# A 48-job attention pipeline: loop written out, row loads moved in the DMA queue, places of side work renumbered

## The reference, cut to what matters

```python
for i in range(6):                                   # x: (4, 512, 256), 16 heads of 16
    xn = adaln(x, cond, n1_w[i], n1_b[i])            # layer norm, then scale and shift from cond
    q, k, v = split(xn @ qkv_w[i].T, 3)              # self attention
    x = x + attn(rope(q), rope(k), v) @ so_w[i].T
    xn = adaln(x, cond, n2_w[i], n2_b[i])            # cross attention on ctx (4, 512, 256)
    q, k, v = xn @ cq_w[i].T, ctx @ ck_w[i].T, ctx @ cv_w[i].T
    x = x + attn(rope(q), rope(k), v) @ co_w[i].T
    xn = adaln(x, cond, n3_w[i], n3_b[i])
    x = x + gelu(xn @ f1_w[i].T + f1_b[i]) @ f2_w[i].T + f2_b[i]     # 256 -> 1024 -> 256
# then, on x0 + x: a mixture of 8 experts (top 2, capacity 640, 256 -> 512 -> 256), added to x
```

## Time and profile before

| what | us |
|---|---|
| median of 3 runs | 4334.48 (4331.78 to 4341.4) |
| the profiled execution | 4337.09 |
| its span, first to last instruction | 4335.3 |
| PE busy | 3833.6 (88% of the span) |
| DVE, ACT, POOL busy | 2841.1, 2498.6, 1148.4 |
| mean granted clock of TensorE | 0.966 of 2.4 GHz |
| SHORT slot in the loop / written out | 63.1 / 62.8 |
| LONG slots | 96.0 to 102.3 |
| everything after the last attention slot (from 3990.6) | 344.7 |

### The profile page before, as it was taken

How to read it: one execution, slowest core, us unless ns; L and a number is a source line. 1 busy time by engine, 2 the same in 40 slices (tenths; PEclk the granted TensorE clock), 3 DMA queues, 4 the chain that set the end, 5 groups by cost and what they waited for, 6 DMA issues and landing times. The chain is left out here.

```text
span 4335.3 us, 66534 instructions
## 1 busy us (share of the span) xinstructions
PE 3833.6 (88%) x19478; PEld 1695.2 (39%) x19478; DVE 2841.1 (66%) x4476; ACT 2498.6 (58%) x4206; POOL 1148.4 (26%) x1280
## 2 busy tenths in 40 slices
PE   3899899899899899899999899999999999897558
PEld 1233344433344433344433344433344433343446
DVE  6788766688666688766688766588766688751411
ACT  1577655577655567655567655567655577654112
POOL 3233222232222232322232322232322232301043
PEclk8999999999999999999999999999999999999779
DMA  5655534445533355433356443456443366521235
GB/s 160 157 153 145 131 80 94 107 137 145 131 81 91 97 145 141 132 90 82 93 150 148 125 95 82 94 145 153 123 99 80 91 171 154 132 54 46 68 103 112
DMA packets 334220, 500.30 MB, mean 115 GB/s; under 512 B 53705, under 2 KB 242257, under 8 KB 333521
## 3 DMA queue, kind: packets, MB, share of 16 engines
q1 hardware_dynamic: 289680, 430.95, 39.0%
q0 software_dynamic: 44160, 64.73, 6.3%
HBM read 278.54 MB, written 222.58 MB: 116 GB/s over the span
## 5 line engine op out<-in xcount | busy, mean ns | idle before, releaser
L908 ACT ACTIVATE prob<-ps 128x512 f32<-128x512 f32 x3072 | 1751.3, 595 | 1249.8 <-PE ps L832 1246.9
L1070 DVE TENSOR_REDUCE negmax<-ps 128x2 f32<-128x1024 f32 x1536 | 1814.8, 1217 | 362.4 <-PE ps L859 332.5
L832 PE MATMUL ps<-qstack,kstack 114*128 114x512 bf16 x3072 | 1144.6, 390 | 118.0 <-ACT prob L908 99.0
L845 PE MATMUL psv<-prob,v 128*32 128x512 f32 x6144 | 826.7, 610 | 0.0
L832 PEld LDWEIGHTS ps<-qstack,kstack 114*128 114x128 bf16 x3072 | 273.9, 97 | 1269.3 <-ACT prob L908 935.7
L859 PE MATMUL ps<-kstack,qstack 49*128 49x512 bf16 x3072 | 487.8, 387 | 78.7 <-DVE negmax L1070 53.3
L677 POOL TENSOR_TENSOR pool_fence<-eps 128x1 f32<-128x1 f32 x288 | 55.2, 192 | 1688.0 <-ACT mrow L975 1026.5
L807 PE MATMUL side<-nT,wf 128*128 128x256 f32 x1536 | 375.0, 387 | 31.9 <-ACT mrow L975 18.3
L1106 DVE TENSOR_SCALAR hT<-side,f1b 128x256 f32<-128x256 f32 x384 | 167.5, 478 | 295.6 <-PE side L807 295.5
L818 PE MATMUL side<-wf,hT 128*128 128x256 f32 x1536 | 350.1, 381 | 3.5 <-DVE x L1113 1.8
L807 PEld LDWEIGHTS side<-nT,wf 128*128 128x128 f32 x1536 | 285.4, 191 | 88.2 <-ACT mrow L975 22.3
(11 more groups left out here) (170 smaller groups left out, 3626.8 us busy)
## 6 DMA issues: line engine op xcount, KB each, us to landing
bounce<-parts SPq DMA_DIRECT2D x480, 256.0 KB, 2.5
qstack<-bounce SPq DMA_DIRECT2D x384, 192.0 KB, 6.1
kstack<-bounce SPq DMA_DIRECT2D x384, 192.0 KB, 6.6
value_sums<-osum SPq DMA_DIRECT2D x192, 256.0 KB, 6.5
bounce<-low SPq DMA_DIRECT2D x96, 256.0 KB, 2.1
hT<-value_sums POOLq DMA_DIRECT2D x96, 256.0 KB, 4.8
nT<-inverse POOLq DMA_DIRECT2D x96, 256.0 KB, 3.8
ctxT<-in_ctxT SPq DMA_DIRECT2D x24, 512.0 KB, 5.3
```

The source lines that it names most:

```text
L832: nc.tensor.matmul(ps2[:, n % RING2, :], kk[0:ROWS, h, kt * P:(kt + 1) * P], q[0:ROWS, h, :], start=True, stop=True).then_inc(s_p2full, 1)
L845: mm = nc.tensor.matmul(psv[32 * i:32 * i + 32, 0, :], v[j % 2][:, kt, (HD + 1) * h:(HD + 1) * h + 32], prob[:, 4 * (u % 2) + i, :], start ...
L908: nc.scalar.activation(prob[:, 4 * (u % 2) + i, :], ps2[:, n % RING2, :], ACT.Exp, scale=HD ** -0.5).then_inc(s_prob, 1)
L1070: nc.vector.tensor_reduce(out_at, ps1[:, 2 * (n % 2):2 * (n % 2) + 2, :], AX, ALU.max, negate=True).then_inc(s_p1free, 1)
```

## The change

Five things change, and what is computed stays the same.

1. `run_slots` writes all 50 slots out; every wait has a constant, and `Place` is gone.
2. The parts: `bounce` has four rows for Q (high, high, mid, low) and four for K (low, mid, high, high). `load_first` and `load_second` read three neighbouring rows each, so a job needs 8 writes, not 12.
3. SP's queue: half 1 of job k is loaded in slot k, behind a new wait for `s_aload`, that is until the chain of job k-2 has loaded everything. The weights come behind those rows: cross weights at k % 8 = 2, F1's at 3, F2's at 4, self weights at 6.
4. POOL: `waited` and `pool_fence` are gone (288 instructions).
5. The tables of places.

```diff
 SHORT = {
-    "M": [25, 0], "HV": [1, 3], "HT": [6, 8], "HQ": [9, 11], "HK": [12, 14], "O": [18, 20],
-    "SPLIT": (14, 16, 19, 21), "PARTS": 23, "RECIP": 8, "NORM": (14, 15),
+    "M": [25, 0], "HV": [1, 3], "HT": [6, 7], "HQ": [8, 9], "HK": [12, 14], "O": [18, 20],
+    "SPLIT": (12, 14, 18, 20), "PARTS": 23, "RECIP": 6, "NORM": (10, 11),
 LONG = {
-    "M": [27, 0], "HV": [1, 3], "HT": [6, 8], "O": [11, 12], "HQ": [14, 15], "HK": [16, 18], "LT": [17, 19],
-    "F1": [20, 21, 22, 23, 24, 25, 26, 27], "F2": [28, 29, 30, 31],
-    "SPLIT": (17, 19, 21, 23), "GELU": (24, 28), "PARTS": 25, "RECIP": 5, "NORM": (9, 10),
+    "M": [27, 0], "HV": [1, 3], "HT": [6, 7], "HQ": [8, 9], "O": [11, 12], "HK": [13, 15], "LT": [16, 17],
+    "F1": [18, 19, 20, 21, 22, 23, 24, 25], "F2": [26, 28, 30, 31],
+    "SPLIT": (13, 15, 18, 20), "GELU": (22, 26), "PARTS": 24, "RECIP": 5, "NORM": (8, 9),
-    "LN_LT": dict(stats=[12, 12, 12, 12], aggregate=13, guess=13, newton=14, tiles=[14, 14, 15, 15]),
+    "LN_LT": dict(stats=[12, 12, 12, 12], aggregate=13, guess=14, newton=14, tiles=[14, 14, 15, 15]),
...
-Q_PARTS = (0, 0, 1, 0, 1, 2)
-K_PARTS = (0, 1, 0, 2, 1, 0)
+PART_ORDER = ((0, 0, 1, 2), (2, 1, 0, 0))
+FIRST_AT, SECOND_AT = (0, 1), (1, 0)
...
-    with eng.Fori(0, NL - 1) as layer:
-        place.layer = layer
-        for k in range(2, 2 + NJ):
-            slot(k, p2=True, p1=True, tail=True, head=True)
...
+    for k in range(JOBS + 2):
+        slot(k, p2=1 <= k <= JOBS, p1=k < JOBS, tail=k >= 2, head=k + 1 < JOBS)
...
                 if tail:
                     write_sums(k - 2, 3)
-                if k % NJ == 2 and p1:
-
-                    sp.wait_ge(s_full, side_done)
-                    load_cross_ffn(k)
                 if head and is_cross(k + 1):
...
+                if tail and p1:
+
+                    sp.wait_ge(s_aload, 64 * (k - 1))
+                if k and p1:
+                    load_first(k, 1)
+                    load_second(k, 1)
+
+                if k % NJ == 2 and p1:
+
+                    sp.wait_ge(s_full, side_done)
+                    load_cross(k)
+                if k % NJ in (3, 4) and p1:
+                    load_ffn(k, k % NJ - 3)
...
-                if head:
-                    load_first(k + 1, 1)
-                    load_second(k + 1, 1)
...
-                wait_sums(pool, place, j)
-                waited()
+                wait_sums(pool, j)
                 pool.dma_start(den[:, :], sums[j % 2][:, HD].rearrange("h (c n) -> h c n", c=P // H)).then_inc(s_den, 16)
```

More of the change, by code:

```diff
@@ L463, in layers @@
         number, start = {}, {}
-        for k in range(-1, 2 * NJ + 2):
+        for k in range(-1, JOBS + 2):
             start[k] = len(number)
@@ L501, in _ @@
         def _(sp):
-            place = Place()
             def at_layer(name, k):
-                layer = place.layer + k // NJ
-                ap = a[name]
-                return ap[bass.ds(layer, 1)] if not isinstance(layer, int) else ap[layer:layer + 1]
+                return a[name][k // NJ:k // NJ + 1]
             def load_self(k):
@@ L535, in write_part @@
-                sp.wait_ge((s_hi, s_mid, s_low)[part], place.jobs(j, 2) + w + 1)
-                for r in range(NPROD):
+                        sp.wait_ge(s_first[hf], FIRST_DMAS * j)
+                        sp.wait_ge(s_second[hf], SECOND_DMAS * j)
+                sp.wait_ge((s_hi, s_mid, s_low)[part], 2 * j + w + 1)
+                for r in range(len(order)):
                     if order[r] == part:
@@ L591, in slot @@
             def slot(k, p2, p1, tail, head):
[L592 removed]
+                side_done = start[k]
                 for g in NORM_WEIGHTS.get(k, {}):
@@ L1083, in side_work @@
                     return
-                wait_filled(dve, place, k, what, c)
+                wait_filled(dve, k, what, c)
                 bank = side[:, 0, :]
```

243 lines of the change are left out of this document (100 added, 143 removed).

## The result

The changed kernel takes **4213.3 us** (4208.2 to 4219.1, 4 runs) against 4333.9 (4331.8 to 4341.4), a ratio of 0.9719, 95% interval 0.9700 to 0.9738. So 121 us are gained where 194 were forecast, and the time lies above the range of 4100 to 4205. The profiled execution took 4208.2, its span is 4206.5.

What follows compares the result with a forecast made beforehand. PE was taken to set slot length, plus its idle times. Gains of 26.6 + 24 + 80.8 + 28.6 + 30 + 10 = 200 us off 4334.5 give 4134.5; with 5.5 given back, 4140 us, range 4100 to 4205.

Steps and rivals of the forecast that it cites:

- terms 4: Other LONG-slot places: M's copy 0.8 us, HQ/HK neighbours 0.3, LT's wait 0.2 gained; 28.6 us, bounds -20 and 58.
- Term 5: SHORT slots: PE's waits of 0.31 and 1.04 us behind ACT's casts go; 30 us, bounds 15 and 33.
- its check: Cross-check of the forecast time by slots: 24 SHORT slots at 61.5 us and 21 LONG at 92.5.
- Terms 1 and 2: Loop written out: waits at four layer turns go, 26.6 us; constants replace counts in registers, 24 us, bounds 14 and 34.
- Term 3: LONG slots: waits at RECIP and NORM go, and the clock's falls behind them; 80.8 us, or 40 if NORM still waits.
- the sign that the prediction gave for being wrong: In the trace after: lower clock in slots that have no wait of the attention's chain, one of several signs; no size given.
- Term 6: Half 1's row loads behind the chain arrive 2.6 us before pass 1 needs them in SHORT slots; cost nothing.
- rows late: Rival: half 1's rows come some 3 us late in 24 SHORT slots, costing 72 us, 4212; chance 0.10.
- straight code stalls: Rival: written-out code stalls 5.5 us in every fourth of 40 slots, giving back 55, 4195; chance 0.04.
- Term 7: Start and ends: slot 47's wait of 5.6 us shrinks, slots 0, 1 and 49 gain; 10 us, bounds 5 to 14.
- the chain stays too slow: Rival: a wait at NORM, place 8 or 10, remains; term 3 shrinks to 40, Term 7 to 5, 4186; chance 0.15.
- The give-back: 5.5 us returned from the gain for small waits of the 0.3 kind from new neighbours, 0.1 in a slot.

Runs made afterwards that it cites:

- Experiment 1: The kernel before with only the layer loop written out and waits on constants, places, parts and row loads as before: 4269.2 us, 0.9834 of the kernel before.
- Experiment 8: Changed kernel with K's chunks at 14 and 15, first cast at 12, guess at 13, all norm tiles at 14 in LONG slots: 4195.4 us, 0.9658.
- experiment 9: Changed kernel with LT at 17 and 18, F1 at 19 to 26, F2 at 28 to 31, gelus at 24 and 28 in LONG slots: 4171.7 us, 0.9596.
- experiment 2: Changed kernel with the old tables of places, all else of the change kept: 4231.6 us, 0.9750 of the kernel before.
- experiment 4: Changed kernel with DVE's two products (NORM) in SHORT slots back at places 14 and 15, not 10 and 11: 4263.1 us, 0.9822.
- (5): Changed kernel with DVE's two products (NORM) in SHORT slots at places 11 and 16, not 10 and 11: 4205.1 us, 0.9686.
- Experiment 7: Changed kernel with chunk M at 22 and the parts at 19 in SHORT slots, so the M rows load earlier: 4185.3 us, 0.9645.
- (11): Changed kernel with six rows of parts in DRAM as before, 192 more writes, all else as changed: 4213.2 us, 0.9703.
- Experiment 12: Changed kernel with M 22, parts 19, products 11 and 16 (SHORT), LT 17 and 18, F1 and F2 later, gelus 24 and 28 (LONG): 4129.4 us, 0.9489.

## Why the prediction was wrong, step by step

The step that failed is the same in terms 4 and 5: each moved step was priced by the wait that it takes away. What the moves add, beside a wait of 1.4 us at LT, was put at 0.1 us in a slot, 5.5 in all, with nothing for a fall of the clock behind them. The runs show 1.27 us in each SHORT slot (DVE's products behind a rope of Q), late M rows at the ends of ten, and 0.78 and 2.07 us in each LONG slot (DVE's tiles behind a rope of K), with a fall of the clock behind them in 19 of 21.

The profiled executions differ by 128.9 us, 65.6 less than the forecast's 194.5. The medians add 7.7 to the miss, since the profiled execution of before lies 2.6 above its median and that of after 5.1 below. The rest is this:

| part of the miss | us |
|---|---|
| SHORT slots without a late row, mostly the new wait, (62.4 - 61.5) x 24 | 21.6 |
| SHORT slots over 62.4 (late M rows, the clock behind) | 15.2 |
| falls of the clock in LONG slots, (94.05 - 92.64) x 19 | 26.8 |
| LONG slots without a fall, 0.14 x 21 | 2.9 |
| start and ends | 6.4 |
| given back already in the forecast, and rounding of its check | -7.2 |

**Terms 1 and 2, the loop.** The edges were right: no DVE wait on "issue" at a turn is left, and slot 10 takes 62.45 with the change. The counts in registers were too low: 41 us (67.8 of the spans less 26.6), outside the bounds of 14 to 34. The step that failed is the comparison of slots 15 and 46 behind LT: it measures how much slower the matmuls' stream is, but with 0.9 for a whole slot it leaves only 4 us for the stretch ahead of LT in all twenty. Experiment 1 shows the place: behind LT it gained 15.2 us, as counted (14), and ahead of LT 25.3. There the attention's chain runs; NORM's waits fall by 13 us, and three falls of the clock are gone. That it is the chain's own waits on counts is likely, not shown.

**Term 3, the chain.** The mechanism was right at both its places. RECIP's wait went by the order of SP's queue and NORM's by the places, and PE does not wait for the products ahead of O in any LONG slot of the loop. Sizes: 80.8 was worked out as all that lies over 94.7, and some of this was the loop's (above), so terms 2 and 3 counted in one sum are the better reading. They were forecast at 99 in LONG slots; with term 4 that makes the 127 of the table, against 97.4. DVE still idles at NORM in ten LONG slots of the loop, 0.2 to 1.45 us, but PE does not see it. The step that failed stands in its words "half what the clock costs behind them": the fall was taken to go with this wait, but it came back behind another. This is the sign that the prediction gave for being wrong: a lower clock in slots that have no wait of the chain.

**Term 4, other places in LONG slots.** M's copy: right, 18.3 to nothing. LT's wait was forecast at 1.4 and is 2.07, with 0.78 ahead of it; the step that followed DVE put the last two tiles at 0.7, and they took 1.67, since one of them stands until POOL's instruction beside it is over (last section). It also did not ask what DVE's backlog does to the scores ahead of LT. The two waits together are 1.4 us over the forecast, within the bound of 3.5. What it triggers was not in the bound at all: the fall of the clock in 19 slots, 26.8 us. Experiment 8 takes most falls away and gets 26 us back; experiment 9 halves them, shortens LT's wait as well, and gets 53 (a slot without a fall takes 91.4 there, not 92.6). That such a slot takes 92.64 in the changed kernel where 92.5 was forecast, in spite of 1.4 us more of these waits, is in part luck: small waits went that the sum did not have. With the old tables (experiment 2) slot 14 has 0.54 us for an exponential and 0.42 and 0.39 for ropes, and 0.3 was counted.

**Term 5, ACT's casts in SHORT slots.** The casts' waits went, 1.35 a slot. But the step asked only what covers ACT; the products that the same table moved from 14 and 15 to 10 and 11 stood only in the rivals, for whether the inverses are there in time, not for whom they hold up. They hold up PE for 1.27 us. SHORT slots gained 27.9 in all, and 26.6 of that is term 1: terms 2 and 5 came to about nothing there. That moving them back is worse (experiment 4) and moving them apart better (5) speaks for their distance from the ropes as what counts. What stood in no step: earlier casts bring half 0's row loads forward, and the M rows' load, whose place did not change, is then issued behind all ten of them, not amid them. Experiment 7 gets 32 us back, of which these waits themselves are 12.4. In experiment 2, with the old places, no SHORT slot has this wait.

**Term 6, half 1's row loads.** Right. In slot 13 (from 1019.2) SP issues the first at 1040.38, 21.2 us in (forecast 21.8), and PE passes unit 8 without a wait, 35.1 us in:

```profile
1033.82 0.58 POOL L658 DMA_DIRECT2D inverse<-recip  x1 [6.65 <-DVE recip L1119]
1040.38 0.32 SPq L525 DMA_DIRECT2D qstack<-bounce  x1
...
1054.32 0.60 PE L824 MATMUL ps<-kstack,qstack 49*128 49x512 bf16 x4
```

The four-row parts are worth nothing that can be told (11). The rivals "rows late" and "straight code stalls" did not come. That the first of them gives 4212 and 4213 was measured is chance: no PE wait for the rows of half 1 is there.

**Term 7, the ends.** 3.6 of 10. Slot 47 still has a wait for the inverses, which moved from O to NORM as the rival "the chain stays too slow" has it:

```profile
3711.37 0.69 DVE L1123 TENSOR_TENSOR hT<-hT,nT 128x512 f32<-128x512 f32 x1 [3.45 <-DMA nT<-inverse]
...
3713.25 0.61 PE L824 MATMUL ps<-kstack,qstack 49*128 49x512 bf16 x2 [3.72 <-DVE negmax L1027]
```

**The give-back and the range.** 5.5 us for "small waits that new neighbours bring" stood for what cost about 60 (21.6, 15.2 and 26.8 above). The sentence on the range gives "about 35 us to each side", and that does not follow from the bounds: their root of squares is 31 us on the side of more gain (10, 29.4 and 3) and 66 on the side of less (10, 40.8, 48.6 and 15). The stated range, 40 and 65 us from 4140, is near that. A root of squares takes the misses as apart, but the three large ones had one source: each edit was costed by the wait that it removes, with DVE and the small DMA load taken as they were. Experiment 12 reaches 0.9489, below the 0.9551 of the forecast, so the size of the gain was there to be had, with other places.

**Still open.** Which of two slots with the same waits has a fall of the clock. In experiment 9, slots 15 and 16 have the same five waits to 0.01 us; the one takes 91.4 and the other 92.95. And why the start is 3.3 us longer with the change: it differs by more between the other kernels (137.7 to 144.1 us to the first exponential of slot 1), and was not followed up. Last, what of experiment 7's gain is in undisturbed slots.

## What to carry to other kernels

When a table of places is changed, cost each moved step twice: for the wait that it removes, and for the engine that it loads at its new place, by laying that engine's instructions out over the next three or four places. In this kernel, steps of the same engine that share neighbouring places (rope, product, rope) are to be spread, even where each would be in time. Look also at what has *not* moved: a small load whose place is unchanged can come to stand behind large ones that were brought forward. And where the clock has fallen behind waits in the trace of before, a new wait at another place must carry a price for a fall as well as its own length.
